# First layer: the pieces of turned probabilities issued by SyncE and ScalarE, and the value product copied at its unit's end

## The reference

```
h = Wqkv z + Winj u                       # 3 * 16 * 64 rows, 512 positions
q, k, v = split(h);  rq = q + r_w_bias
score = rq . k / 8                        # per head, 512 x 512
prob  = softmax(score)
attn  = prob . v                          # summed over the 512 keys
x     = Wo attn + bo + z
out   = (x - mean) * rsqrt(var + 1e-5)    # over the 256 rows
```

## Time and profile before

| | us |
|---|---|
| median of 3 runs | 3449.86 |
| lowest and highest | 3442.28, 3452.65 |
| profiled execution | 3459.09 |
| its span | 3456.2 |
| mean granted TensorE clock in it | 0.945 |

### The profile page before, as it was taken

The page is one execution under the profiler, slowest core; times in us unless marked ns, Lnnn a source line. Parts: engine busy times, 40 slices in busy tenths (PEclk is TensorE's granted clock), DMA queues, the critical chain, the costliest instruction groups (busy, mean ns, idle before and its releaser), DMA issues. The chain is left out here.

```text
span 3456.2 us, 55559 instructions
## 1 busy us (share of the span) xinstructions
PE 3132.7 (91%) x20384; PEld 2403.1 (70%) x20384; DVE 2360.5 (68%) x3589; ACT 1741.3 (50%) x4185; POOL 725.6 (21%) x1279
## 2 busy tenths in 40 slices
PE   7998999989998996789999997589999999699998
PEld 6776777777776774556666664277787788488885
DVE  5776756766775672899999999257777888542213
ACT  4454444544453542455565553247777777532222
POOL 2444445445554441000000000011101111000000
PEclk9999999999999997899999998889999999899999
DMA  7668866776795754545454444120011110310004
GB/s 243 208 214 251 243 182 185 196 209 185 210 235 156 201 150 174 124 109 119 111 123 116 105 110 110 42 81 14 26 49 64 44 44 29 107 44 18 25 13 166
DMA packets 179677, 434.79 MB, mean 126 GB/s; under 512 B 52912, under 2 KB 61104, under 8 KB 154960
## 3 DMA queue, kind: packets, MB, share of 16 engines
q1 hardware_dynamic: 120256, 262.17, 28.4%
q0 software_dynamic: 41216, 138.47, 14.0%
q10 hardware_dynamic: 17936, 30.59, 2.5%
HBM read 233.95 MB, written 62.91 MB: 86 GB/s over the span
## 5 line engine op out<-in xcount | busy, mean ns | idle before, releaser
L759 DVE TENSOR_REDUCE l_nmax<-l_bank 128x1 f32<-128x512 f32 x512 | 316.9, 680 | 264.5 <-PE l_bank L467 264.5
L281 POOL DMA_DIRECT2D l_probT<-l_prob x896 | 441.7, 501 | 87.0 <-DVE l_prob L781 71.6
L590 ACT ACTIVATE l_prob<-l_bank,l_nmax 128x512 f32<-128x512 f32 x512 | 344.9, 689 | 112.6 <-DVE l_nmax L759 96.4
L492 PE MATMUL l_bank<-l_probT,l_v 128*64 128x256 f32 x2048 | 270.0, 419 | 81.5 <-DMA l_probT<-l_prob 57.9
L781 DVE STREAM_TRANSPOSE l_prob<-l_prob 128x1024 f32<-128x1024 f32 x256 | 314.3, 1228 | 17.1 <-DVE l_acc L802 9.5
L433 PE MATMUL l_bank<-l_x_hi,l_w_hi 128*128 128x256 f32 x1024 | 298.9, 292 | 19.0 <-DVE l_x_lo L850 11.1
L433 PE MATMUL l_bank<-l_x_hi,l_w_lo 128*128 128x256 f32 x1024 | 291.8, 285 | 0.0
L433 PE MATMUL l_bank<-l_x_lo,l_w_hi 128*128 128x256 f32 x1024 | 291.4, 285 | 0.0
L492 PEld LDWEIGHTS l_bank<-l_probT,l_v 128*64 128x64 f32 x2048 | 156.9, 149 | 185.9 <-issue 60.0
L1820 DVE TENSOR_TENSOR_SCAN l_kv<-l_wx,l_kv 128x2056 f32<-128x2056 f32 x64 | 283.8, 4434 | 3.1 <-DVE l_sxc L1941 1.5
L2394 ACT ACTIVATE l2a_sc<-l2a_sc,l2a_nmax 128x256 f32<-128x256 f32 x512 | 254.8, 508 | 41.0 <-DVE l2a_nmax L2510 41.0
(11 more groups left out here) (352 smaller groups left out, 8099.7 us busy)
## 6 DMA issues: line engine op xcount, KB each, us to landing
l_probT<-l_prob SPq DMA_DIRECT2D x1152, 64.0 KB, 2.8
l_vb<-vd SPq DMA_DIRECT2D x64, 1024.0 KB
l_probT<-l_prob POOLq DMA_DIRECT2D x896, 64.0 KB, 2.4
l_w_hi<-kept_w_hi POOLq DMA_DIRECT2D x24, 1024.0 KB, 10.7
l_w_lo<-kept_w_lo POOLq DMA_DIRECT2D x24, 1024.0 KB, 14.8
l_wv_hi<-kept_wv_hi POOLq DMA_DIRECT2D x12, 1024.0 KB, 6.7
l_wv_lo<-kept_wv_lo POOLq DMA_DIRECT2D x12, 1024.0 KB, 9.5
kept_w_hi<-l_w_hi SPq DMA_DIRECT2D x8, 1024.0 KB, 10.6
```

Source lines behind the costliest of these rows:

```text
L281: eng.dma_start(probT[i % RING][r * SQ:(r + 1) * SQ, g, :, :, :, :], prob[i % RING][g * SQ:(g + 1) * SQ, r * IT:(r + 1) * IT, :, :, :]).th ...
L492: mm = pe.matmul(s.ap[own, f * ROWS:(f + 1) * ROWS], v[l][:, pair % 2, j, own], half[:, :, :, j, h, :], start=j == 0, stop=j == IT - 1)
L590: act.activation(prob[i % RING][:, :, it % 2, h, :].rearrange("p (q t) s -> p t q s", q=Q), s.ap[:, :].rearrange("p (t q s) -> p t q s", t ...
L759: dve.tensor_reduce(nmax[:, n % 2, it, h:h + 1], s.ap[:, :], AX.X, ALU.max, negate=True).then_inc(max_ready, 1)
```

## The change

GpSimd no longer issues pieces. ScalarE issues its seven of each half: those of the second half of unit n - 1 after the first four exponentials of unit n, those of the first half of n after the second four. The semaphores `moved_pool` become `moved_act`. The copy of the value product (`weighed`) moves from the start of a unit to the end of the unit before, ahead of the values' copies instead of behind them. On GpSimd the scaling comes ahead of the spreading. SyncE's nine pieces stay; in the changed file the lines from the GpSimd loop on carry numbers lower by 3.

```diff
-        moved_pool = [kept.enter_context(nc.semaphore(f"kept_moved_pool{i}")) for i in range(RING)]
+        moved_act = [ph.sem(f"moved_act{i}") for i in range(RING)]
@@ half_moved
-            eng.wait_ge(moved_pool[i % RING], 16 * (len(MOVES) - BY_SP) * (i // RING + 1))
+            eng.wait_ge(moved_act[i % RING], 16 * (len(MOVES) - BY_SP) * (i // RING + 1))
@@ block.gpsimd
                 for n in range(HALF + 2):
-                    if 0 < n <= HALF:
-                        spread_sums(n - 1)
                     if n > 1:
                         scale_outputs(n - 2)
                     if 0 < n <= HALF:
-                        move(pool, n - 1, 1, MOVES[BY_SP:], moved_pool)
+                        spread_sums(n - 1)
                     if n >= HALF:
                         continue
-                    move(pool, n, 0, MOVES[BY_SP:], moved_pool)
@@ block.scalar
                 for n in range(HALF):
                     bp, pair, l = where(n)
-                    if n > 1:
-                        weighed(n - 2)
                     exponentials(n, (0, 1))
+                    if n:
+                        move(act, n - 1, 1, MOVES[BY_SP:], moved_act)
                     if n + 1 < HALF:
                         queries(n + 1)
...
                     exponentials(n, (2, 3))
+                    move(act, n, 0, MOVES[BY_SP:], moved_act)
                     if n == 0:
                         split_wo()
...
+                    if n:
+                        weighed(n - 1)
                     if n + 1 < HALF:
                         values(n + 1)
...
-                weighed(HALF - 2)
+                move(act, HALF - 1, 1, MOVES[BY_SP:], moved_act)
                 outputs(HALF - 2)
                 sums(HALF - 1)
                 weighed(HALF - 1)
```

## The result

The changed kernel takes 3674.5 us as the median of four runs (3666.9 to 3680.2), the kernel before 3451.3 beside it (3442.3 to 3454.1): a ratio of 1.065, 95% interval 1.063 to 1.067. Slower was forecast, but 3480, and the time lies far above the range. The profiled execution took 3679.1 (span 3677.1). The first layer's 64 units, from the first score matmul of unit 0 to the end of the last value product, grew from 1281.9 to 1507.9 us in the two profiled executions: 226.0, which is the whole difference (223.3 by the medians).

A forecast was written before the change was run, and what follows sets the result against it. TensorE was taken as the bound, ScalarE as half idle. Later units -14, units 19 and 35 -20, first batch pair +42, batch turns +22: +30 us on 3459.1, so 3480 as a median; 8-in-10 range 3420 to 3560, likeliest 3465 to 3520.

The forecast's parts named there:

- Issue time, run-ahead and the short unit: On ScalarE: 0.59 us an issue, issuing ahead of computing, and some 15.8 us for a unit without value projection.
- The first rival: ScalarE hides its blocks: at 0.45 us an issue, units without value projection stay near 14.8; 3394 us; faster had 0.22.
- the last rival: ScalarE's and SyncE's issues block each other: first block 2 us longer in each of 64 units, 3610 us; chance 0.07.
- What the removal gives: GpSimd's load starts some 9 us earlier in unit 21; unit 22's stall goes, 1.5 us of stall left for ScalarE's first block.
- units 19 and 35: First-layer units lengthened by SyncE's late pieces; an earlier load was to free both, -20 us.
- the rival in which the stall only moves: The load meets ScalarE's first block in unit 21, so the 5.5 us stay: 3528 us; chance 0.15.
- The price of the blocks: First layer: ScalarE's two 4.2 us blocks a unit delay query copy, maxima and output projection.
- The twelve fours: Groups of four units after the first batch pair: 73.75 us each with ScalarE's blocks where 70.8 would do.
- the first pair: First batch pair, 329.2 us before: raw-weight rounding waits behind ScalarE's second block and nothing hides that chain; +42 us.
- the batch turns: Units 14, 15, 30, 31, 46, 47: input roundings delayed 3 to 4 us each, with the late unit behind; +22 us.
- The value product's copy: On ScalarE, put ahead of the values' copies: costs nothing, since TensorE delivers in that order.
- The sum: Whole kernel: -14 - 20 + 42 + 22 = +30 us, giving 3489 profiled and 3480 as a median.

The follow-up runs named there:

- late loads: Changed kernel, with GpSimd holding each load of kept weights back until the second half of the unit before has landed: 3583.4 us (1.039).
- the two kernels without loads: Changed kernel and kernel before, each with its loads of kept weights cut to one partition of 128: 3553.8 us (1.030) and 3379.0 us (0.980).

## Why the prediction was wrong

**Issue time, run-ahead and the short unit: right.** 0.61 us where 0.59 was taken; the block in unit 21 begins 0.1 us after the last maximum; unit 22 takes 15.7 where 15.8 was walked, though its like (units 18 to 46 and 58) go up to 17.3. The first rival needed 0.55 or less, the last one issues lengthened by each other; neither is there. The section of the Trainium skill named with the last rival (Perfetto Trace Analysis, "DMA Instruction — HWDGE (DVE, Sync)") speaks of VectorE and SyncE as the two that share the descriptor generator, not of ScalarE, so it was not that rival in full.

**What the removal gives: the step that failed.** It said that the load, starting some 9 us earlier, would mostly have landed before the late half has to move, left 1.5 us of stall for ScalarE's first block, and took 20 us back in units 19 and 35: -69 in all against the loads' cost. Measured without and with loads, that cost went from 77.0 to 130.4: +53 (+48 by the medians). The load did start 9 us earlier. What I got wrong is that ScalarE's part of the late half has no other time than the load's. On GpSimd its pieces were issued ahead of the load, from 2.5 us into the unit; on ScalarE they come from 3.6 us on, little later, but the load now starts at 0.4, 3.2 us ahead of them. I also left out the 2 MB loads of remainder 3: they caused no stall before, so no row pointed at them, but with nothing ahead of them on GpSimd they cross the same block and cost 5.5 us in unit 23 (28.0 against 22.4) and 0.4 to 7.0 in the others from unit 19 to 59. So the rival in which the stall only moves came true, and in two units of each four instead of one: 7.8 us in unit 21 (5.98 of wait and 1.8 of lower clock) instead of 5.5. It had 0.15. Its counterargument, seven pieces and not sixteen, is what the landing refutes. Units 19 and 35 gave back 3.1 and 4.4 us, not 20; with late loads, which the early start was to better, they gave 7.2 and 9.9.

**The price of the blocks: right mechanism, too small.** The twelve fours, the first pair and the batch turns made 35 + 42 + 22 = 99; the two kernels without loads say 172.6. By units (us longer on the changed kernel, both without loads; the fours' 35 are divided over units 16 to 63):

| units | in the prediction | measured |
|---|---|---|
| 0 to 12 | 42 | 54.8 |
| batch turns (13 to 15, 30 to 32, 46 to 48) | 22 + 4 | 37.9 |
| 16 to 29, 33 to 45, 56 to 59 | 23 | 45.3 |
| 49 to 55 | 5 | 18.7 |
| 60 to 63 | 3 | 15.8 |

A clean four pays 5.3 (76.0 against 70.7), not 2.95: its units are 1.0, 1.0, 1.5 and 1.7 us longer than without blocks, where I had 0.4, 0.4, 1.1 and 1.05, and it is the output projection that waits. Two small numbers make 0.45 of the 0.6 that the first two miss: first issue to query copy is 4.5 us, not 4.2; and in the earlier trace rows the query remainder starts 0.86 before the output remainder, while I counted its duration. In the first pair the chain of the roundings is real (39 us come back when they go first). Units 49 to 55, where the first norm's work is added, and the last four I didn't walk by themselves. Without loads TensorE waits 14 us longer in units 49 to 55 (28.2 against 14.0): 5.9 more for the output remainder and 8.3 more for steps of the norm. In the last four the wait for the output remainder grew from 2.6 to 9.3. What makes the rest of these units' 34 us stays open.

**The value product's copy:** nothing, as said, on the kernel before.

**The sum** thus missed by 122 in the loads and 74 in the blocks. Its bound for the stall, 5.5 us in one unit of four, was taken from the one stall that the trace of before showed, not from what a late half costs behind each load that is sent ahead of it.

## What to carry to other kernels

When an issuer is freed, ask which of its other transfers now start earlier, and list for each what still has to be issued behind them: the order of issue decided here which unit stalls, and by how much. A compute engine that issues pays each issue in full once it has caught up with its last wait (ScalarE stood 3.50 us of its 4.5 us block in unit 21), so walk the first block through to the engine that bounds, with start-to-start times. A big load that crosses short deadlines is worth dividing: on the kernel before, dividing it gave 37 us, and sending it early cost 127.

## What the hardware showed beside that

GpSimd's scaling takes 1.28 us in all 64 units of the kernel before. In the changed one it takes 2.9 in 15 of them, 11 of these in the first batch pair, each begun 0.5 us after VectorE began to subtract raw weights or inputs. Groups of GpSimd's instructions in the first pair (busy, mean ns, then idle before), then the timeline of GpSimd and VectorE in unit 4, of the changed kernel:

```profile
L391 POOL TENSOR_TENSOR l_oT<-l_oT,l_rT 128x512 f32<-128x512 f32 x15 | 37.1, 2475 | 314.6 <-ACT l_oT L623 314.6
```

```profile
155.33 2.92 POOL L391 TENSOR_TENSOR l_oT<-l_oT,l_rT 128x512 f32<-128x512 f32 x1 [25.74 <-ACT l_oT L623]
...
154.80 2.29 DVE L813 TENSOR_TENSOR l_w_lo<-first_anx,l_w_hi 128x2048 fp32r<-128x2048 f32 x1 [6.55 <-ACT l_w_hi L642]
```

GpSimd ends 1.16 us after VectorE does (158.25 against 157.09), near its own 1.28, and in all 15 it ends 1.12 to 1.16 after: it stood until VectorE was done. The Trainium skill, SBUF — State Buffer, "SBUF: two separate sides", has the two engines share a pair of ports that one holds for a whole instruction; the trace agrees. By the list of waits, nothing in the first pair waited for it.
